# A decoder layer on one core: ScalarE copies the second turned head of each pair out of its bank

## The chip, the cores and the metric

One core of a Trainium2 chip runs the whole program. The metric is the device time in microseconds, the median of three runs of the same program. Beside it stands the profile of one execution, whose span (first to last instruction) is a little shorter than that execution's time.

## What is computed

A pre-norm decoder layer on x of (8, 256, 128) with a context of (8, 512, 128): self-attention with 16 heads of 64, one cross-attention head of 128, and a feed-forward part with quantised weights and activations, all in float32 to the outside.

```python
x = x + attn(layernorm(x), norm_scale, wq, wk, wv, w_out, b_out)      # 16 heads, softmax over 256 keys
x = x + xattn(k=ctx, v=ctx, q=layernorm(x), Wk, Wv, bv, Wq, bq, Wo, bo)  # softmax over 512 keys
x = x + ffn(layernorm(x), w1, b1, w2, b2)                             # 512 hidden, uint8 activations, int8 weights

def attn(x, ...):
    h = rmsnorm(x) * norm_scale
    q, k, v = (einsum('bsd,dhe->bshe', h, w) for w in (wq, wk, wv))
    p = softmax(einsum('bqhd,bkhd->bhqk', q * 64 ** -0.5, k))
    return einsum('bqhe,hed->bqd', einsum('bhqk,bkhd->bqhd', p, v), w_out) + b_out
```

## The kernel before

The program is written engine by engine: each engine has its own list of instructions in a fixed order, and semaphores tie the lists together. Nothing is scheduled by a compiler.

**The loop.** The work goes over 8 batches of 8 pairs of heads. One call of `step` on each engine stands for one pair j of batch b, with g = 8b + j as the running number of the pair. Batch 0 is written out ("first"), batches 1 to 6 are a loop of three rounds over two batches ("mid"), batch 7 is written out ("last"). After it comes a tail with the last batch's cross attention and the feed-forward part.

**One pair on the engines.** The heads are handled at different distances, so that every engine has work from several pairs in hand. In step g, TensorE turns (transposes) the scaled probabilities of the pair's two heads through the bank `turned_bank`, each turn four 128x128 matmuls on line 494; makes queries and keys of pair g+4 (L453 to L455, bank `q_bank`); projects the output of pair g-2 (`project_out`, L510, bank `acc_bank`); multiplies values of pair g-1 (L503, `o_bank`); and makes the scores of pair g+3 (L484, `score`). ScalarE takes exponentials of pair g+2 (L768), rounds q (`q_hi`, `split_hi`), copies `o_bank` to `oT`. VectorE takes the negated maxima of pair g+2 (L951), copies the turned probabilities to `pT` (L958), splits off q's remainder (`q_lo`, L943) and inverts sums (L955). GpSimd multiplies the probabilities by the inverted sums (L1324). All copies by ScalarE have line 759.

**Between them, side tasks.** A table gives up to three places in a step (0, 1, 2) to side tasks that go through `side_bank`: TH turns the normalised rows of the next batch, V0 and W1 to W3 make its values (`v_sb`), TC turns the context, TX turns the rows for the cross attention (ScalarE copies `x2T_hi`, VectorE then `x2T_lo`), QX, SX0 and SX1 its queries and scores (VectorE `x_negmax`, ScalarE `x_prob`), PX0 and PX1 turn its probabilities (ScalarE `x_pT_hi`, VectorE `x_pT_lo`), UX and OX finish it. TX has place 1 of pair 2. It is in batches 1 to 7, not in batch 0.

**The turned heads.** `turned_bank` is one bank. Both heads of a pair pass through it in turn: the even head's turn, its copy to `pT`, the odd head's turn, its copy. Both copies are VectorE's, counted by one semaphore, `pT_done`, and each turn waits for the copy before. In the last three pairs of the last batch (`late`) the turns go through three banks, `turned_bank` and the two `q_bank`s, by `turned_in`, and `copied_before` gives the count of copies that a turn must wait for. A pair's `values` in the next step read both copies.

**The order in a step.** On ScalarE: exponentials of the first head, side task of place 0, exponentials of the second head, `q_hi`, `oT`, side tasks of places 1 and 2. On VectorE: maxima of the first head, copy of the even turned head, maxima of the second, side task of place 0, inverse of the first sums, copy of the odd turned head, `q_lo`, side task of place 1, inverse of the second sums, side task of place 2. On TensorE: turn of the even head, q and k, side task of place 0, `project_out`, turn of the odd head, `values`, side task of place 1, scores, side task of place 2. At the end of pair 1 ScalarE also rounds the context rows (`c_rows_hi`), and in the last batch it scales the feed-forward weights there.

**The tail.** VectorE rounds and sums the feed-forward weights after its last copy, then adds the residual (L1002) from `acc_bank`, on which the rest of the cross attention hangs.

Of the kernel before, what the change touches and what calls it, by code (L numbers as in the profile page):

```python
# [71 lines left out]
def decoder_layer(nc, x, ctx_in, norm_scale, wq, wk, wv, w_out, b_out, xWk, xWv, xbv, xWq, xbq,  # L72
                  xWo, xbo, w1, b1, w2, b2, out):
    B, S, D = x.shape
    H, E = wq.shape[1], wq.shape[2]
# [5 lines left out]
    PAIRS = H // 2  # L81
# [32 lines left out]
    def wait(eng, sem, value):  # L114

        if isinstance(value, int) and value <= 0:
            return
        eng.wait_ge(sem, value)

    with ExitStack() as ctx:  # L120
# [6 lines left out]
        def sem(name):  # L127
            return ctx.enter_context(nc.semaphore(name))
# [56 lines left out]
        pT = sb("pT", [P, 4, QT, S])  # L185
# [102 lines left out]
        rinv_done = sem("rinv_done")  # L288
        prob_done = sem("prob_done")
        pT_raw = sem("pT_raw")  # L290
        pT_done = sem("pT_done")
        o_raw = sem("o_raw")
        o_done = sem("o_done")
        acc_raw = sem("acc_raw")
# [87 lines left out]
        def late(kind, j):  # L382

            return kind == "last" and j >= PAIRS - 3

        def turned_in(kind, j, r):
            if late(kind, j):
                return (turned_bank, *q_banks)[(2 * (j - PAIRS + 3) + r) % 3]
            return turned_bank

        def copied_before(kind, g, j, r):

            return 2 * g + r - (2 if late(kind, j) and (j > PAIRS - 3 or r) else 0)

        block = ctx.enter_context(nc.Block())

# [53 lines left out]
        def _(pe):  # L450
# [122 lines left out]
            def step(kind, b, parity, i, j):  # L573
                g = b * PAIRS + j
                pe.wait_ge(prob_done, 2 * g + 1)
                wait(pe, pT_done, copied_before(kind, g, j, 0))
                turn_probs(2 * j % 8, turned_in(kind, j, 0))
                if ahead(kind, j, 4):
                    if kind == "first" and j == 0:
                        pe.wait_ge(wqk_lo_done, 4)  # L580
                    project_qk((j + 4) % PAIRS, parity if j < PAIRS - 4 else 1 - parity, q_banks[j % 2])
                if task := side_at(kind, j, 0):
                    side(kind, b, 1 - parity, i, task)

                if not (kind == "first" and j < 1):
                    wait(pe, o_done, g - 1)
                if not (kind == "first" and j < 2):
                    if j == 2:
                        wait(pe, x1_done, b)
                    if kind == "first" and j == 2:  # L590
                        pe.wait_ge(load_wo, 16)
                    project_out((j - 2) % PAIRS)
                pe.wait_ge(prob_done, 2 * g + 2)
                pe.wait_ge(pT_done, copied_before(kind, g, j, 1))
                turn_probs(2 * j % 8 + 1, turned_in(kind, j, 1))
                if not (kind == "first" and j < 1):
                    if j == 1:
                        pe.wait_ge(side_free, side_index(kind, b, "W2") + 1)
                    if j == 5:
                        pe.wait_ge(side_free, side_index(kind, b, "W3") + 1)  # L600
                    if late(kind, j):
                        pe.wait_ge(pT_done, 2 * g)
                    slot = 2 * (j - 1) % 4
                    values((j - 1) % PAIRS, (slot, slot + 1), 1 - parity if j == 0 else parity)
                if task := side_at(kind, j, 1):
                    side(kind, b, 1 - parity, i, task)
                if ahead(kind, j, 3):
                    pe.wait_ge(q_lo_done, g + 4)
                    pe.wait_ge(exp_done, 2 * g + 6)
                    scores((j + 1) % 2)  # L610
                if task := side_at(kind, j, 2):
                    side(kind, b, 1 - parity, i, task)
# [29 lines left out]

            pe.wait_ge(pT_done, B * H)
            values(PAIRS - 1, (2, 3), LAST % 2, score_bank[0])
            pe.wait_ge(o_done, B * PAIRS - 1)
            project_out(PAIRS - 2)
# [108 lines left out]
        def _(act):  # L757
# [3 lines left out]
            def split_hi(parity, bank):  # L761

                return copy(q_hi[:, parity].rearrange("p r q -> p (r q)"), bank[:]).then_inc(q_hi_done, 1)
# [41 lines left out]
            def step(kind, b, parity, i, j):  # L805
                g = b * PAIRS + j
# [9 lines left out]
                if ahead(kind, j, 4):  # L816
                    act.wait_ge(q_raw, g + 5)
                    split_hi(j % 2, q_banks[j % 2])
                if not (kind == "first" and j < 1):
                    act.wait_ge(o_raw, g)  # L820
                    copy(oT[:, (j - 1) % 2], o_bank[:, 0:S]).then_inc(o_done, 1)
# [118 lines left out]
        def _(dve):  # L940
# [13 lines left out]
            def invert_sums(slot):  # L954
                nc.vector.reciprocal(rinv[:, slot], rowsum[:, slot]).then_inc(rinv_done, 1)  # L955

            def keep_turned(slot, bank):
                nc.vector.tensor_copy(pT[:, slot].rearrange("p k q -> p (k q)"), bank[:]).then_inc(pT_done, 1)  # L958

            def statistics(k, src, n):  # L960

# [119 lines left out]
            def step(kind, b, parity, i, j):  # L1081
                g = b * PAIRS + j
# [8 lines left out]
                if kind == "mid" and j == PAIRS - 1:  # L1091
                    aggregate(2, b, *PLAIN_NORM)
                dve.wait_ge(pT_raw, 2 * g + 1)
                keep_turned(2 * j % 4, turned_in(kind, j, 0))
                if kind == "first" and j == 0:
                    dve.wait_ge(exp_done, 3)
                    invert_sums(2)
# [24 lines left out]
                    residual(b, 1 - parity)  # L1122
                if kind == "mid" and j == PAIRS - 2:
                    statistics(2, x2_of(b), b)
                dve.wait_ge(pT_raw, 2 * g + 2)
                keep_turned(2 * j % 4 + 1, turned_in(kind, j, 1))
                if prepare and j == 0:
                    if kind == "first":
                        dve.wait_ge(load_x[1], 16)
# [293 lines left out]
```

## Time and profile before

| | us |
|---|---|
| median of 3 runs | 385.61 (385.21 to 386.19) |
| the profiled execution, its time | 386.2 |
| its span | 384.4 |
| TensorE matmul busy | 370.2 (96%) |
| VectorE busy | 325.8 (85%) |
| ScalarE busy | 259.6 (68%) |
| GpSimd busy | 174.3 (45%) |

The three runs lie within 0.3% of each other. The profiled execution is near the highest of them. A busy share says how long an engine had an instruction in hand, not whether anybody waited for it. Matmuls overlap one another on TensorE, so their start times tell more than their durations: a 128x128 matmul's row shows about 0.28 us, and the next one starts about 0.11 us later. A line with "PEld" is the weight load ahead of a matmul. What stands in square brackets at a row's end is how long the engine stood idle before it and who ended that.

### The profile page before, as it was taken

What the parts mean: (1) busy time and instruction counts of PE and PEld (TensorE: products, weight loads), DVE (VectorE), ACT (ScalarE), POOL (GpSimd) and SP (SyncE); (2) the same over time, 40 slices, a digit from 0 to 9 for tenths busy, and PEclk for the clock granted to TensorE, in tenths of its full rate; (3) what the DMA queues carried; (4) which work ended last, traced back from release to release, by engine and by line L of the source; (5) the groups of instructions that cost most, each with busy time, mean ns of one, the idle gap of its engine ahead of it and who ended that gap; (6) DMA issues with size and microseconds to landing.
All of it is one profiled execution on the core that took longest, in us unless ns stands there. A gap on an engine that the chain in (4) does not pass through costs nothing.

```text
span 384.4 us, 9135 instructions
## 1 busy us (share of the span) xinstructions
PE 370.2 (96%) x3034; PEld 288.4 (75%) x3034; DVE 325.8 (85%) x790; ACT 259.6 (68%) x812; POOL 174.3 (45%) x188
## 2 busy tenths in 40 slices
PE   8889999999999999999999999999999998999975
PEld 7768778778878877788777888787778876676422
DVE  3888879988998899879998899879987997876995
ACT  3867676766777567766677667756876668725664
POOL 2574435553555445545555454634555543521000
PEclk9999999999999999999999999999999999999999
DMA  7500000001000100001000100000000100000003
GB/s 231 166 15 2 2 0 2 3 3 41 2 1 3 42 0 0 0 0 41 0 0 0 41 0 0 0 30 10 0 0 0 27 2 2 2 2 0 2 0 109
DMA packets 7190, 7.50 MB, mean 20 GB/s; under 512 B 1280, under 2 KB 5120, under 8 KB 7168
## 3 DMA queue, kind: packets, MB, share of 16 engines
q1 hardware_dynamic: 6736, 6.69, 5.6%
q10 hardware_dynamic: 432, 0.52, 0.5%
q8 instruction: 13, 0.21, 0.2%
q14 instruction: 9, 0.07, 0.1%
HBM read 6.16 MB, written 1.05 MB: 19 GB/s over the span
## 4 chain that ended last, share of the span: by engine, by line
PE 81%; DVE 8%; ACT 7%; issue 3%; POOL 1%; POOLq 0%; DVEq 0%; ACTq 0%
PE o_bank L503 15%; PE turned_bank L494 14%; PE score L484 14%; PE acc_bank L510 7%; PE side_bank L453 4%; ACT prob L768 4%; PE q_bank L453 3%; PE q_bank L455 3%; PE q_bank L454 3%; PE side_bank L454 3%; PE side_bank L455 3%; PE side_bank L564 3%; DVE h_max L1280 2%; PE score L618 2%; PE side_bank L557 2%
## 5 line engine op out<-in xcount | busy, mean ns | idle before, releaser
L1324 POOL TENSOR_TENSOR prob<-prob,rinv 128x512 f32<-128x512 f32 x128 | 133.4, 1044 | 156.7 <-DVE rinv L955 156.4
L768 ACT ACTIVATE prob<-score,negmax 128x256 f32<-128x256 f32 x252 | 116.9, 473 | 36.2 <-DVE negmax L951 34.4
L958 DVE COPY pT<-turned_bank 128x512 f32<-128x512 f32 x124 | 84.1, 679 | 12.5 <-PE turned_bank L494 10.9
L951 DVE TENSOR_REDUCE negmax<-score 128x2 f32<-128x512 f32 x126 | 85.8, 682 | 3.4 <-PE score L484 1.1
L494 PE MATMUL turned_bank<-ident,prob 128*128 128x128 f32 x496 | 76.8, 277 | 0.3 <-DVE pT L958 0.2
L503 PE MATMUL o_bank<-pT,v_sb 128*64 128x256 f32 x504 | 68.3, 392 | 0.0
L494 PEld LDWEIGHTS turned_bank<-ident,prob 128*128 128x128 f32 x496 | 56.3, 141 | 9.1 <-issue 0.6
L768 ACT ACTIVATION_READ_ACCUMULATOR prob<-score,negmax 128x1 f32 x252 | 51.4, 204 | 0.0
L943 DVE TENSOR_TENSOR q_lo<-q_bank,q_hi 128x512 fp32r<-128x512 f32 x63 | 43.3, 689 | 6.8 <-ACT q_hi L759 4.9
L484 PE MATMUL score<-q_hi 64*128 64x256 f32 x252 | 42.3, 330 | 3.8 <-ACT prob L768 3.2
L503 PEld LDWEIGHTS o_bank<-pT,v_sb 128*64 128x64 f32 x504 | 30.5, 136 | 19.6 <-issue 9.2
L484 PEld LDWEIGHTS score<-q_hi 64*128 64x128 f32 x252 | 23.9, 184 | 25.8 <-issue 14.5
L453 PE MATMUL q_bank<-ht_hi,wqk_hi 128*128 128x256 f32 x124 | 40.2, 324 | 0.0
L510 PE MATMUL acc_bank<-wo_sb,oT 128*128 128x128 f32 x256 | 39.1, 276 | 0.0
L759 ACT ACTIVATE q_hi<-q_bank 128x512 fp32r<-128x512 f32 x63 | 38.1, 605 | 0.2
L759 ACT ACTIVATE v_sb<-side_bank 128x512 f32<-128x512 f32 x32 | 19.1, 598 | 26.6 <-PE side_bank L455 26.6
L510 PEld LDWEIGHTS acc_bank<-wo_sb,oT 128*128 128x128 f32 x256 | 34.7, 191 | 1.8 <-ACT oT L759 0.4
L484 PE MATMUL score<-q_lo,q_hi 64*128 64x256 f32 x252 | 35.9, 278 | 0.0
L484 PE MATMUL score<-q_hi,q_lo 64*128 64x256 f32 x252 | 35.8, 277 | 0.0
L455 PE MATMUL q_bank<-ht_hi,wqk_lo 128*128 128x256 f32 x124 | 34.9, 281 | 0.0
L454 PE MATMUL q_bank<-ht_lo,wqk_hi 128*128 128x256 f32 x124 | 34.8, 280 | 0.0
L759 ACT ACTIVATE oT<-o_bank 128x256 f32<-128x256 f32 x63 | 24.5, 388 | 6.2 <-PE o_bank L503 5.9
(249 smaller groups left out, 652.9 us busy)
## 6 DMA issues: line engine op xcount, KB each, us to landing
c_sb<-in_ctx_dram SPq DMA_DIRECT2D x8, 256.0 KB, 2.7
x_sb<-in_x_dram SPq DMA_DIRECT2D x8, 128.0 KB, 2.5
out_dram<-xn_all SPq DMA_DIRECT2D x4, 256.0 KB, 2.4
big<-in_L_attn_wk_dram ACTq DMA_DIRECT2D x2, 256.0 KB, 5.1
big<-in_L_attn_wq_dram SPq DMA_DIRECT2D x2, 256.0 KB, 5.6
big<-in_L_attn_wv_dram SPq DMA_DIRECT2D x2, 256.0 KB, 6.2
wo_sb<-in_L_attn_w_out_dram SPq DMA_DIRECT2D x1, 512.0 KB, 7.5
w_sb<-in_L_ffn_w_dram SPq DMA_DIRECT2D x2, 256.0 KB, 4.5
```

Source lines behind the costliest of these rows:

```text
L453: nc.tensor.matmul(dst, lhs_hi, rhs_hi, start=True, stop=False)
L454: nc.tensor.matmul(dst, lhs_hi, rhs_lo, start=False, stop=False)
L455: return nc.tensor.matmul(dst, lhs_lo, rhs_hi, start=False, stop=True)
L484: last = nc.tensor.matmul(banks[r][:, t * S:(t + 1) * S], query[rows, parity, 0, t * P:(t + 1) * P], key[rows, parity, 1, :], start=(n == ...
L494: last = nc.tensor.transpose(bank[:, kt * S + t * P:kt * S + (t + 1) * P], prob[:, slot, t, kt * P:(kt + 1) * P], ident[:])
L503: last = nc.tensor.matmul(bank[r * E:(r + 1) * E, 0:S], v_sb[:, vp, kt, h * E:(h + 1) * E], pT[:, slots[r], kt, :], start=(kt == 0), stop= ...
L510: last = nc.tensor.matmul(acc_bank[:, t * D:(t + 1) * D], oT[:, pair % 2, t * P:(t + 1) * P], wo_sb[:, pair, :], start=(pair == 0 and t == 0),
L759: return nc.scalar.activation(dst, src, ACT.Copy, **kw)
L768: last = nc.scalar.activation(prob[:, slot, t, :], banks[r][:, t * S:(t + 1) * S], ACT.Exp, bias=negmax[:, slot, t:t + 1], scale=1.0, accu ...
L951: nc.vector.tensor_reduce(negmax[:, slot], banks[r][:].rearrange("p (t k) -> p t k", k=S), X_AXIS, ALU.max, negate=True).then_inc(max_done, 1)
L958: nc.vector.tensor_copy(pT[:, slot].rearrange("p k q -> p (k q)"), bank[:]).then_inc(pT_done, 1)
L1324: nc.gpsimd.tensor_tensor(prob[:, slot], prob[:, slot], rinv[:, slot].unsqueeze(2).to_broadcast([P, QT, S]), ALU.mult).then_inc(prob_done, 1)
```

## The change

The copy of each pair's odd turned head moves from VectorE's list to ScalarE's. There it stands behind `q_hi` and ahead of `oT`. The even head's copy stays with VectorE. The one semaphore `pT_done` becomes two, `pT_even` (VectorE's copies) and `pT_odd` (ScalarE's), each of which rises by one per pair. `copied_before` returns two counts, and each turn, each late `values` and the last one wait for both. The operations and what they write are otherwise the same.

```diff
         def copied_before(kind, g, j, r):
 
-            return 2 * g + r - (2 if late(kind, j) and (j > PAIRS - 3 or r) else 0)
+
+            heads = r - (2 if late(kind, j) and (j > PAIRS - 3 or r) else 0)
+            return g + (heads + 1) // 2, g + heads // 2
...
                 pe.wait_ge(prob_done, 2 * g + 1)
-                wait(pe, pT_done, copied_before(kind, g, j, 0))
+                first, second = copied_before(kind, g, j, 0)
+                wait(pe, pT_even, first)
+                wait(pe, pT_odd, second)
                 turn_probs(2 * j % 8, turned_in(kind, j, 0))
...
                 if ahead(kind, j, 4):
                     act.wait_ge(q_raw, g + 5)
                     split_hi(j % 2, q_banks[j % 2])
+                act.wait_ge(pT_raw, 2 * g + 2)
+                copy(pT[:, 2 * j % 4 + 1].rearrange("p k q -> p (k q)"), turned_in(kind, j, 1)[:]).then_inc(pT_odd, 1)
                 if not (kind == "first" and j < 1):
                     act.wait_ge(o_raw, g)
                     copy(oT[:, (j - 1) % 2], o_bank[:, 0:S]).then_inc(o_done, 1)
...
                 if kind == "mid" and j == PAIRS - 2:
                     statistics(2, x2_of(b), b)
-                dve.wait_ge(pT_raw, 2 * g + 2)
-                keep_turned(2 * j % 4 + 1, turned_in(kind, j, 1))
```

ScalarE's list in the first batch of the loop, from the rounding of the context rows at the end of pair 1 to the end of pair 2, before:

```order
L759 ACTIVATE c_rows_hi<-c_sb 128x512
L809 ISA
L768 ACTIVATE prob,rowsum<-score,negmax 128x256 x2
L759 ACTIVATE ht_hi<-side_bank,scale_d 128x256
L814 REGISTER_ALU
L768 ACTIVATE prob,rowsum<-score,negmax 128x256 x2
L817 REGISTER_ALU
L759 ACTIVATE q_hi<-q_bank 128x512
L759 ACTIVATE oT<-o_bank 128x256
L782 REGISTER_ALU
L759 ACTIVATE x2T_hi<-side_bank 128x256
```

and the same stretch of the changed kernel, where the line numbers of later code are higher by 9:

```order
L768 ACTIVATE c_rows_hi<-c_sb 128x512
L818 ISA
L777 ACTIVATE prob,rowsum<-score,negmax 128x256 x2
L768 ACTIVATE ht_hi<-side_bank,scale_d 128x256
L823 REGISTER_ALU
L777 ACTIVATE prob,rowsum<-score,negmax 128x256 x2
L826 REGISTER_ALU
L768 ACTIVATE q_hi<-q_bank 128x512
L828 REGISTER_ALU
L768 ACTIVATE pT<-turned_bank 128x512
L768 ACTIVATE oT<-o_bank 128x256
L791 REGISTER_ALU
```

The copy to `pT`, with a register operation for its wait, has come in between `q_hi` and `oT`; `x2T_hi` follows `oT` as before.

VectorE's list from pair 2's `ht_lo` to pair 3's copy of the even turned head, before:

```order
L1012 SCALAR_TENSOR_TENSOR ht_lo<-side_bank,scale_d,ht_hi 128x256
L955 RECIPROCAL rinv<-rowsum 128x2
L1125 REGISTER_ALU
L958 COPY pT<-turned_bank 128x512
L1134 REGISTER_ALU
L943 TENSOR_TENSOR q_lo<-q_bank,q_hi 128x512
L943 TENSOR_TENSOR x2T_lo<-side_bank,x2T_hi 128x256
L955 RECIPROCAL rinv<-rowsum 128x2
L1087 ISA
L951 TENSOR_REDUCE negmax<-score 128x2
L1093 REGISTER_ALU
L958 COPY pT<-turned_bank 128x512
```

and in the changed kernel:

```order
L1023 SCALAR_TENSOR_TENSOR ht_lo<-side_bank,scale_d,ht_hi 128x256
L966 RECIPROCAL rinv<-rowsum 128x2
L1143 REGISTER_ALU
L954 TENSOR_TENSOR q_lo<-q_bank,q_hi 128x512
L954 TENSOR_TENSOR x2T_lo<-side_bank,x2T_hi 128x256
L966 RECIPROCAL rinv<-rowsum 128x2
L1098 ISA
L962 TENSOR_REDUCE negmax<-score 128x2
L1104 REGISTER_ALU
L969 COPY pT<-turned_bank 128x512
```

The first of the two `pT` copies has gone from the piece; `x2T_lo`, the maxima and the copy of pair 3's even head keep their order.

## Rows read from the trace of the kernel before

**Rows 1.** The page, busy time, share of the span and instructions of each engine
```profile
PE 370.2 (96%) x3034; PEld 288.4 (75%) x3034; DVE 325.8 (85%) x790; ACT 259.6 (68%) x812; POOL 174.3 (45%) x188
```

**Rows 2.** The page, the chain that ended last, shares by engine
```profile
PE 81%; DVE 8%; ACT 7%; issue 3%; POOL 1%; POOLq 0%; DVEq 0%; ACTq 0%
```

**Rows 3.** Groups of instructions: shapes, count, busy us, mean ns, idle before, releaser
```profile
L958 DVE COPY pT<-turned_bank 128x512 f32<-128x512 f32 x124 | 84.1, 679 | 12.5 <-PE turned_bank L494 10.9
...
L759 ACT ACTIVATE v_sb<-side_bank 128x512 f32<-128x512 f32 x32 | 19.1, 598 | 26.6 <-PE side_bank L455 26.6
```

**Rows 4.** Timeline, middle batch, pairs 1 to 3: start, duration, ScalarE then VectorE
```profile
149.00 0.60 ACT L759 ACTIVATE v_sb<-side_bank 128x512 f32<-128x512 f32 x1 [1.40 <-PE side_bank L455]
149.50 0.62 ACT L759 ACTIVATE c_rows_hi<-c_sb 128x512 fp32r<-128x512 f32 x1
...
152.71 0.41 ACT L759 ACTIVATE oT<-o_bank 128x256 f32<-128x256 f32 x1
152.97 0.43 ACT L759 ACTIVATE x2T_hi<-side_bank 128x256 fp32r<-128x256 f32 x1
154.59 0.48 ACT L768 ACTIVATE prob<-score,negmax 128x256 f32<-128x256 f32 x1 [1.20 <-DVE negmax L951]
...
149.95 0.67 DVE L958 COPY pT<-turned_bank 128x512 f32<-128x512 f32 x1
...
152.88 0.69 DVE L943 TENSOR_TENSOR q_lo<-q_bank,q_hi 128x512 fp32r<-128x512 f32 x1
153.49 0.41 DVE L943 TENSOR_TENSOR x2T_lo<-side_bank,x2T_hi 128x256 fp32r<-128x256 f32 x1
...
154.48 0.68 DVE L958 COPY pT<-turned_bank 128x512 f32<-128x512 f32 x1
```

**Rows 5.** Timeline, TensorE, second turns of pairs 2 and 3
```profile
150.18 0.61 PE L510 MATMUL acc_bank<-wo_sb,oT 128*128 128x128 f32 x4
...
150.74 0.14 PEld L494 LDWEIGHTS turned_bank<-ident,prob 128*128 128x128 f32 x1
150.78 0.30 PE L494 MATMUL turned_bank<-ident,prob 128*128 128x128 f32 x1
...
155.51 0.25 PEld L494 LDWEIGHTS turned_bank<-ident,prob 128*128 128x128 f32 x2
155.62 0.27 PE L494 MATMUL turned_bank<-ident,prob 128*128 128x128 f32 x1
```

**Rows 6.** Timeline, oT and the next first turn: a middle batch, the first batch
```profile
179.02 0.38 ACT L759 ACTIVATE oT<-o_bank 128x256 f32<-128x256 f32 x1
...
179.80 0.20 PEld L494 LDWEIGHTS turned_bank<-ident,prob 128*128 128x128 f32 x2
...
48.70 0.39 ACT L759 ACTIVATE oT<-o_bank 128x256 f32<-128x256 f32 x1
...
49.40 0.20 PEld L494 LDWEIGHTS turned_bank<-ident,prob 128*128 128x128 f32 x2
```

**Rows 7.** Timeline, last batch: pair 3's first copy and second turn, pair 4's PX0
```profile
323.55 0.68 DVE L958 COPY pT<-turned_bank 128x512 f32<-128x512 f32 x1
...
324.39 0.25 PEld L494 LDWEIGHTS turned_bank<-ident,prob 128*128 128x128 f32 x2
...
328.63 0.20 PEld L557 LDWEIGHTS side_bank<-ident,x_prob 128*128 128x128 f32 x2 [0.37 <-ACT x_prob L779]
```

**Rows 8.** Timeline, last batch, pair 5: last exponentials, oT, project_out's weights
```profile
335.59 0.49 ACT L768 ACTIVATE prob<-score,negmax 128x256 f32<-128x256 f32 x1
...
336.27 0.38 ACT L759 ACTIVATE oT<-o_bank 128x256 f32<-128x256 f32 x1
...
336.71 0.30 PEld L510 LDWEIGHTS acc_bank<-wo_sb,oT 128*128 128x128 f32 x2
```

**Rows 9.** Timeline, tail: the last projection and VectorE's residual
```profile
342.59 1.26 PE L510 MATMUL acc_bank<-wo_sb,oT 128*128 128x128 f32 x8
...
343.99 0.42 DVE L1002 TENSOR_TENSOR x_sb<-acc_bank,xb_sb 128x256 f32<-128x256 f32 x1
```

More of the change, by code:

```diff
@@ L290, in decoder_layer @@
         pT_raw = sem("pT_raw")
-        pT_done = sem("pT_done")
+        pT_even = sem("pT_even")
+        pT_odd = sem("pT_odd")
         o_raw = sem("o_raw")
@@ L593, in step @@
                 pe.wait_ge(prob_done, 2 * g + 2)
-                pe.wait_ge(pT_done, copied_before(kind, g, j, 1))
+                first, second = copied_before(kind, g, j, 1)
+                wait(pe, pT_even, first)
+                wait(pe, pT_odd, second)
                 turn_probs(2 * j % 8 + 1, turned_in(kind, j, 1))
@@ L601, in step @@
                     if late(kind, j):
-                        pe.wait_ge(pT_done, 2 * g)
+                        pe.wait_ge(pT_even, g)
+                        pe.wait_ge(pT_odd, g)
                     slot = 2 * (j - 1) % 4
@@ L641, in _ @@
             over_batches(pe, step)
-            pe.wait_ge(pT_done, B * H)
+            pe.wait_ge(pT_even, B * PAIRS)
+            pe.wait_ge(pT_odd, B * PAIRS)
             values(PAIRS - 1, (2, 3), LAST % 2, score_bank[0])
@@ L955, in invert_sums, with keep_first_turned @@
                 nc.vector.reciprocal(rinv[:, slot], rowsum[:, slot]).then_inc(rinv_done, 1)
-            def keep_turned(slot, bank):
-                nc.vector.tensor_copy(pT[:, slot].rearrange("p k q -> p (k q)"), bank[:]).then_inc(pT_done, 1)
+            def keep_first_turned(slot, bank):
+                nc.vector.tensor_copy(pT[:, slot].rearrange("p k q -> p (k q)"), bank[:]).then_inc(pT_even, 1)
             def statistics(k, src, n):
@@ L1093, in step @@
                 dve.wait_ge(pT_raw, 2 * g + 1)
-                keep_turned(2 * j % 4, turned_in(kind, j, 0))
+                keep_first_turned(2 * j % 4, turned_in(kind, j, 0))
                 if kind == "first" and j == 0:
```

## Prediction
> **What bounds the kernel now.** I read the page from the top: busy shares, then the chain that ended last, then the groups, and after that the timeline of one middle batch and of the last batch. TensorE is busy for 370.2 of 384.4 us, VectorE for 325.8 and ScalarE for 259.6 [rows 1]; the chain that ended last runs over PE for 81% and over VectorE and ScalarE for 15% [rows 2]. So VectorE's load is no price by itself: taking work from it gives time only where TensorE waits for VectorE, and giving work to ScalarE costs time only where TensorE ends up waiting for ScalarE. In the middle batches I looked for such places by the start times on PE. One is left: the second turn of pair 2. Four L510 matmuls begin at 150.18 and run 0.61 us in all, 0.28 each, so they start (0.61 - 0.28) / 3 = 0.11 apart and the turn could start at 150.62; it does at 150.78, its weights loaded at 150.74 [rows 5], **0.16 us** late. It waited for VectorE's copy of the first head, which ended at 149.95 + 0.67 = 150.62 [rows 4]; the release takes 0.12 us. At pair 3 the load (155.51) goes 0.11 ahead of its matmul (155.62), without a wait.
>
> **The moved copy.** 64 copies of 128x512 leave VectorE, 0.679 us each (43.5 us), and 64 come to ScalarE. The trace has no ScalarE copy of turned_bank; the nearest row is ScalarE's copy of another bank in the same shape, v_sb, 0.598 us [rows 3], and after it the next one starts 0.50 later (149.00, then the row after it at 149.50) [rows 4]. I take a slot of 0.49, with 0.48 and 0.52 as near bounds and VectorE's 0.68 as the far one. Most of the 64 have cover: ScalarE stands idle until VectorE has the next maxima, as for 1.20 us before 154.59, or until TensorE has a side task ready, as for 1.40 us before 149.00 [rows 4], and the copy goes into that hole. The Trainium skill ("ScalarE: Activation LUTs", Rules for kernel authors) tells one to use VectorE and not ScalarE for plain arithmetic, which speaks against this change. The rows here do not bear it out for a float32 bank: 0.598 us against 0.679. The same page (What ACT_TABLE_LOAD costs) has 186 ns + 0.833 ns per element, less 93 ns of overlap; an estimate from it is a slot of 0.52, and with it the sum below would be 0.2 us higher.
>
> **Who waits for the copy itself.** The next pair's first turn writes the same bank, so it now waits for ScalarE. The tightest places are where no side task stands between scores and turn. In pair 7 of a middle batch the new copy takes the place of oT, which starts at 179.02; it ends at 179.62, ScalarE's releases reach PE after 0.06 us (oT ends at 336.27 + 0.38 = 336.65, and the load that waits for it goes at 336.71 [rows 8]), so it is ready at 179.68 and the load goes at 179.80 [rows 6]. In pair 6 of the first batch it is ready at 48.70 + 0.60 + 0.06 = 49.36 and the load goes at 49.40 [rows 6]. Margins of 0.12 and 0.04: no cost, but thin. In the pairs with more side work between, the same subtraction leaves more. The extra wait instructions on PE (a second semaphore, six register operations in the loop body) stand in a queue that runs ahead of the array; I cost them at nothing, and if that cover were missing, rival 3 has the price.
>
> **What is queued behind the copy on ScalarE: pair 2.** Here the hole comes too late. From v_sb at 149.00 to x2T_hi at 152.97 ScalarE works back to back; the new copy goes in ahead of oT, so x2T_hi starts 0.49 later and ends at 152.97 + 0.43 + 0.49 = 153.89 [rows 4]. VectorE splits x2T (x2T_lo) before it takes the next scores' maxima and before it copies pair 3's first turned head. Before, x2T_lo started at 153.49, kept by q_lo (152.88 + 0.61); now it waits for x2T_hi, until about 153.93, a slip of 0.44 (I take 0.04 for the release to VectorE, a little under the 0.06 to PE above). Maxima and copy follow without a gap: the copy of pair 3's first head ends at 154.48 + 0.68 + 0.44 = 155.60, and its release reaches PE at 155.72. PE's load for the second turn went at 155.51 [rows 5]: now 155.72. A load that was waited for has its matmul 0.04 behind (150.74, 150.78), so the turn starts at 155.76 in place of 155.62: **0.14 us later**. The 0.16 that pair 2's second turn can gain, because VectorE's queue ahead of it holds one copy less, is inside this figure and is no gain: the chain from v_sb on ScalarE to the second turn of pair 3 is fixed by ScalarE, whatever PE does in between. Behind it PE is the bound again: pair 3's copy ahead of oT finds ScalarE's hole before x_prob. Six middle batches: 6 x 0.14 = **0.84 us**. Bounds: with slots of 0.48 and 0.52, 0.8 and 1.0; with a slip wholly hidden, -6 x 0.16 = -1.0; with VectorE's 0.68 as the slot, 6 x 0.33 = 2.0.
>
> **The last batch.** Pair 2 repeats this, with PE a little earlier against VectorE. The copy of pair 3's first head ends at 323.55 + 0.68 = 324.23, with a slip of 0.43 at 324.66, load at 324.78 in place of 324.39 [rows 7]. That is 0.39 for the load and 0.32 for the matmul, and further on it grows: in pair 4 PE waited 0.37 us for x_prob (load at 328.63 [rows 7]), and x_prob hangs on VectorE's maxima, which stand behind q_lo and so behind the whole slipped ScalarE row: **0.43 us**. In pair 5 PE loads project_out's weights at 336.71, 0.06 after oT's end at 336.27 + 0.38. oT started when its matmuls were done; ScalarE is free from about 336.04, shortly before the last exponential's end at 335.59 + 0.49. Now the odd copy starts there and oT 0.49 behind it, at 336.53: **0.26 us** more [rows 8]. Against that VectorE gets its copies off its queue before the weight sums: the first residual operation of the tail started at 343.99 right behind them, though acc_bank's last matmul ended at 343.85 [rows 9]; it can start at 343.91: **-0.08 us**. In the first batch I cost the move at nothing: there is no x2T in it, and its tightest turn has the margin of 0.04 above.
>
> **Sum.** 0.84 + 0.43 + 0.26 - 0.08 = 1.45 us. The profiled execution took 386.2 us (span 384.4 and 1.8 around it), so 387.65 for a like one; it is the highest of the three runs shown, and on their median of 385.61 I forecast **387.1 us**. That is 0.38% slower; a difference of about 0.3%, 1.16 us, is what a measurement of this kernel can tell from no change.
>
> **Rivals.** (1) *The slip is hidden and the stall comes back.* If x2T_hi doesn't hold VectorE up, because the copy's slot on ScalarE is short, PE keeps what it gains at pair 2's second turn. Pair 3's second turn was ready for its load at 155.16 + 0.12 = 155.28, 0.23 ahead; with PE 0.16 earlier 0.07 of that is left. With a slip under 0.07 the time would be 385.61 - 6 x 0.16 - 0.08 = 384.6, faster than before. For it: ScalarE's work on a bank is shorter than VectorE's. Against: the slip is a whole slot, and v_sb shows 0.50. (2) *It cancels.* The matmul would then be at 155.32 plus the slip, against 155.62: a slip of 0.30 costs a middle batch nothing, one of 0.2 gives it 0.1, and the last batch keeps some 0.5 us: 385.5 to 386.1, the middle 385.8. For it: my slip of 0.44 comes from rows with two decimals, and a middle batch costs only 0.14; 0.14 less of slip is enough. (3) *The first turns wait too.* If the copy takes longer than v_sb's, or the added waits and register operations on ScalarE and PE take room, the margins of 0.12 and 0.04 go. It decides at those margins. With 0.2 us more per copy, pair 7 loses 0.08 in each of 7 batches, three bare pairs of the first batch 0.16 each, and pair 2 loses 0.2 in each of 7: 0.56 + 0.48 + 1.4 = 2.4 us more than forecast, 389.5; with half of that 388.3, which I take as this case's time. Against: ScalarE's rows at this shape are 0.60 and 0.62 [rows 4]. (4) *The change doesn't do what it says*: the order shows all 64 copies on ScalarE and the rest unmoved, so this has no share.
>
> **How the numbers follow.** Forecast 0.55, no change (2) 0.27, stall gained (1) 0.07, first turns wait (3) 0.11. The forecast's own spread is that of a slot between 0.40 and 0.60: 0.09 less or 0.11 more in each middle batch and about 0.2 either way in the last, 386.4 to 388.0. The range takes that in, the case of no change, and the near half of (3) with most of the way to the far bound of the slot: 385.3 to 388.5. Slower by over 0.3% is above 386.77: most of the forecast's case (0.45 of its 0.55) and (3), 0.56. Faster by over 0.3% is below 384.45: only a lucky part of (1), 0.03. Within it 0.41.
>
> **What would show it.** In the profile after: the ScalarE group of pT copies, x64 or 62, near 0.6 us; in each middle batch x2T_lo starting 0.04 behind x2T_hi's end and waiting for it, not for q_lo; a wait of about 0.2 to 0.3 us on PE for VectorE's pT copy at the second turn of pair 3, and none at pair 2's; in the last batch a longer wait of PE for x_prob's successors and about 0.3 us before project_out in pair 5. VectorE near 282 us busy and ScalarE near 298. The forecast is wrong if oT and x2T_hi don't start later, if the wait at pair 3 is missing, or if the first turns wait for ScalarE.

## The result, and the profile after

The changed kernel takes **386.67 us** (median of 9 executions, 386.18 to 387.07) against 385.39 us for the kernel before beside it (9 executions, 385.10 to 386.19). The ratio is 1.0032, 95% interval 1.0021 to 1.0042: 0.3% slower, 1.3 us. A second comparison gave 386.45 against 385.73, ratio 1.0023 (1.0013 to 1.0033). The forecast was 387.1 us, slower, with a range from 385.3 to 388.5. Its sign and its main places were right; one size, that of the middle batches, was twice too large, and three small waits at first turns were not in it. The experiments end at a kernel that is 2 us faster than before.

Busy time and the chain that ended last, of the kernel after (compare [rows 1, 2]):

```profile
PE 370.4 (96%) x3034; PEld 287.6 (75%) x3034; DVE 288.5 (75%) x726; ACT 289.2 (75%) x876; POOL 174.6 (45%) x188
...
PE 81%; ACT 7%; DVE 6%; issue 3%; POOL 1%; POOLq 0%; DVEq 0%; ACTq 0%
```

VectorE's busy time fell by 37.3 us and ScalarE's rose by 29.6, and the time went up. TensorE's line is the same as before to 0.2 us. A balance of 288 to 289 us each looks better than 326 to 260, and says nothing about the end.

The groups of the two copies after (compare [rows 3]; columns: shapes and count | busy, mean ns | idle before, releaser), and VectorE's split of q:

```profile
L954 DVE TENSOR_TENSOR q_lo<-q_bank,q_hi 128x512 fp32r<-128x512 f32 x63 | 43.4, 691 | 41.4 <-ACT q_hi L768 41.4
...
L969 DVE COPY pT<-turned_bank 128x512 f32<-128x512 f32 x62 | 42.4, 684 | 10.1 <-PE turned_bank L497 10.0
...
L768 ACT ACTIVATE pT<-turned_bank 128x512 f32<-128x512 f32 x62 | 38.3, 618 | 1.2 <-PE turned_bank L497 1.2
```

62 copies of turned_bank are on each engine (and two of q_bank). ScalarE's take 618 ns against VectorE's 684. What VectorE was given back it spends waiting: 41.4 us ahead of q_lo, for ScalarE's q_hi, where it was 6.8 us before.

Next, ScalarE, VectorE and TensorE in pairs 2 and 3 of the middle batch that [rows 4, 5] show, after the change (timeline: start, duration, engine, operation, [idle before, releaser]):

```profile
148.04 0.60 ACT L768 ACTIVATE v_sb<-side_bank 128x512 f32<-128x512 f32 x1 [0.93 <-PE side_bank L458]
148.53 0.62 ACT L768 ACTIVATE c_rows_hi<-c_sb 128x512 fp32r<-128x512 f32 x1
149.05 0.47 ACT L777 ACTIVATE prob<-score,negmax 128x256 f32<-128x256 f32 x1
149.21 0.61 PE L513 MATMUL acc_bank<-wo_sb,oT 128*128 128x128 f32 x4
149.66 0.60 PE L497 MATMUL turned_bank<-ident,prob 128*128 128x128 f32 x4
...
151.69 0.64 ACT L768 ACTIVATE pT<-turned_bank 128x512 f32<-128x512 f32 x1
152.17 0.43 ACT L768 ACTIVATE oT<-o_bank 128x256 f32<-128x256 f32 x1
152.43 0.44 ACT L768 ACTIVATE x2T_hi<-side_bank 128x256 fp32r<-128x256 f32 x1
152.90 0.42 DVE L954 TENSOR_TENSOR x2T_lo<-side_bank,x2T_hi 128x256 fp32r<-128x256 f32 x1 [0.34 <-ACT x2T_hi L768]
153.31 0.67 DVE L962 TENSOR_REDUCE negmax<-score 128x2 f32<-128x512 f32 x1
153.90 0.68 DVE L969 COPY pT<-turned_bank 128x512 f32<-128x512 f32 x1
154.04 0.61 PE L513 MATMUL acc_bank<-wo_sb,oT 128*128 128x128 f32 x4
154.66 0.42 PEld L497 LDWEIGHTS turned_bank<-ident,prob 128*128 128x128 f32 x4 [0.20 <-POOL prob L1333]
154.69 0.63 PE L497 MATMUL turned_bank<-ident,prob 128*128 128x128 f32 x4
```

The stall at pair 2's second turn is gone: the turn starts at 149.66, as soon as the projection's four matmuls, 0.11 apart from 149.21 on, let it (149.21 + 0.44 = 149.65). At pair 3 there is a new one: projection at 154.04, the turn at 154.69 where 154.48 was possible. On the way stands what the prediction named: the copy's slot ahead of oT (151.69 to 152.17, 0.48 us), a late x2T_hi, x2T_lo waiting for it, maxima, copy, load. The releaser printed at 154.66, GpSimd's prob, had ended at 154.52; VectorE's copy ended at 153.90 + 0.68 = 154.58 and is the last. The two ends lie close together, and both hang on x2T_lo, so this was worth a second look: TensorE's sequencer had a semaphore instruction open there, for the two counts of copies and not for prob. It ran from 153.494 to 154.630, 0.05 us behind the copy's end, and the load went 0.025 us after it. So the name beside a wait for several semaphores must be read against the rows.

**Where the time went**, in nanoseconds. I paired the matmuls of the two traces one by one and took the difference of their start times at the borders of the stages; each column is what a stage adds to or takes from the kernel before. (The middle column is the mean of six periods of the loop; the border ahead of it lies before the first batch's last pair. The first and the last column are not the change: up to 12 us each trace has its own start-up, and the feed-forward part its own clock. That the start-up is not the change's can be seen from the column itself: the kernels "behind x2T" and "oT first" have all odd copies on ScalarE too, and differ from the kernel before by 31 and 177 ns there, not by 1.1 us.)

```
kernel             to 12 us   first   one middle   last    tail    feed-
                   (not the   batch   batch, x6    batch   norm    forward
                   change)
after              -1165      +40     +70          +728    -37     +547
after, again       -1142      +20     +49          +702    -47      -11
both on VectorE     -449      -13     -56           +21    +37       +4
pair 1 alone       -1102        0     -173          +20    +30       -7
pair 2 alone       -1435       +7     +110         +461    +37     +460
all but pair 2     -1033      +42     -172         +293    -36       +4
behind x2T           -31     +234     +344         +837    -46      -10
oT first (last)     -177      +14     +52          +440    -47       -3
pair 1, scalings 6   +24      -20     -173        -1214   +422       -5
pair 1, scalings 5  -300       -6     -173        -1213    +26       -3
```

The change itself is 0.04 + 6 x 0.07 + 0.73 - 0.04 = 1.15 us in the first trace and 0.97 us in the second, against 1.28 and 0.72 us between the medians. For all ten rows the sum without the two outer columns lies within 0.5 us of the difference of the medians. The 0.55 us in the feed-forward part is variation: the second trace of the same kernel doesn't have it. The granted clock tells them apart (stretch and its length, busy us of PE, PEld, DVE, ACT and POOL with counts, PEclk, DMA share, GB/s). After:

```profile
370.00:384.00 14.00, 8.64 (x39) 4.04 (x38) 9.01 (x26) 6.68 (x10) 0.00 (x0) 0.87 0.21 73
```

After, again:

```profile
370.00:384.00 14.00, 7.68 (x38) 3.63 (x38) 8.84 (x26) 6.45 (x10) 0.00 (x0) 1.00 0.22 75
```

The same number of matmuls is busy for 8.64 us at a mean granted clock of 0.87 and 7.68 at 1.00, that is, at the higher of TensorE's two levels (2.4 GHz) for all of the stretch.

### The profile page after: what moved, and what is told of

It reads as the page before. It is cut to its first block, busy times and chain, and to the rows that moved or that the text cites. A ratio compares the mean times of both kernels' runs of the same rounds, so it can differ in the third digit from the quotient of the medians.

```text
span 384.9 us, 9156 instructions
## 1 busy us (share of the span) xinstructions
PE 370.4 (96%) x3034; PEld 287.6 (75%) x3034; DVE 288.5 (75%) x726; ACT 289.2 (75%) x876; POOL 174.6 (45%) x188
## 4 chain that ended last, share of the span: by engine, by line
PE 81%; ACT 7%; DVE 6%; issue 3%; POOL 1%; POOLq 0%; DVEq 0%; ACTq 0%
PE o_bank L506 15%; PE turned_bank L497 14%; PE score L487 14%; PE acc_bank L513 7%; ACT prob L777 4%; PE side_bank L456 4%; PE q_bank L456 3%; PE q_bank L458 3%; PE q_bank L457 3%; PE side_bank L457 3%; PE side_bank L458 3%; PE side_bank L567 3%; DVE h_max L1289 2%; PE side_bank L560 2%; PE score L626 1%
## 5 line engine op out<-in xcount | busy, mean ns | idle before, releaser
L954 DVE TENSOR_TENSOR q_lo<-q_bank,q_hi 128x512 fp32r<-128x512 f32 x63 | 43.4, 691 | 41.4 <-ACT q_hi L768 41.4
L969 DVE COPY pT<-turned_bank 128x512 f32<-128x512 f32 x62 | 42.4, 684 | 10.1 <-PE turned_bank L497 10.0
L768 ACT ACTIVATE pT<-turned_bank 128x512 f32<-128x512 f32 x62 | 38.3, 618 | 1.2 <-PE turned_bank L497 1.2
```

What stands on the lines that cost most here:

```text
L768: return nc.scalar.activation(dst, src, ACT.Copy, **kw)
L954: return nc.vector.tensor_tensor(dst, whole, hi.bitcast(F32), ALU.subtract)
```

## The experiments

My theory, A, was: the copies don't cost by their sum; pair 1's gives time back, pair 2's takes it away through x2T_hi, and pair 5's in the last batch through oT. The rival, B: the extra semaphore, or the copies' mass on ScalarE, slows every pair a little. (Where a later kernel has another alternative, its expectation says so.) Each kernel is a variant of the changed one in which a predicate says whose second copy is ScalarE's; VectorE makes the others where it did before, and releases the second semaphore. Each is compared with executions of the kernel before that were made beside it, in three sets, whose medians are 385.76, 385.73 and 385.42 us.

**Both copies on VectorE, two semaphores.** This leaves only the change's bookkeeping.

```diff
+        def odd_by_act(kind, j):
+            return False
...
+                if odd_by_act(kind, j):
                     act.wait_ge(pT_raw, 2 * g + 2)
                     copy(...).then_inc(pT_odd, 1)
...
+                if not odd_by_act(kind, j):
+                    dve.wait_ge(pT_raw, 2 * g + 2)
+                    keep_second_turned(2 * j % 4 + 1, turned_in(kind, j, 1))
```

> Both copies stay with VectorE, and only the semaphore is split in two, so that TensorE has the changed kernel's waits and register operations. Theory A (the time comes from the place of the copy in ScalarE's and VectorE's queues): no change from the kernel before, 385.4 us within 0.3. Theory B (the added waits on TensorE cost): up to the whole 1.3 us of the change, 386.7.

Measured: 385.53 us against 385.76, ratio 0.9996 (0.9987 to 1.0005). The extra waits cost nothing that the comparison can tell. The trace even shows a gain, 0.056 us in every middle batch, at one place, pair 2's second turn:

```profile
149.37 0.68 DVE L974 COPY pT<-turned_bank 128x512 f32<-128x512 f32 x1
149.59 0.61 PE L517 MATMUL acc_bank<-wo_sb,oT 128*128 128x128 f32 x4
150.10 0.42 PEld L501 LDWEIGHTS turned_bank<-ident,prob 128*128 128x128 f32 x4
150.10 0.55 PE L501 MATMUL turned_bank<-ident,prob 128*128 128x128 f32 x3
```

The copy ends at 150.05 and the turn's load goes 0.05 later; before, it ended at 150.62 and the load went at 150.74 [rows 4, 5], 0.12 later. What differs is a wait instruction of its own on TensorE's sequencer, a kind of record that the timeline leaves out. From the trace, in ns (start, duration):

```
before:            150667   51  EVENT_SEMAPHORE
                   150744  138  LDWEIGHTS turned_bank<-ident,prob
two semaphores:    149490   51  EVENT_SEMAPHORE
                   150100  138  LDWEIGHTS turned_bank<-ident,prob
after, pair 5 of    39518   51  EVENT_SEMAPHORE
the first batch:    39593  142  LDWEIGHTS turned_bank<-ident,prob
after, pair 3 of   153494 1136  EVENT_SEMAPHORE
a middle batch:    154655  138  LDWEIGHTS turned_bank<-ident,prob
```

Where the semaphore instruction has not begun when the copy ends, it starts 0.04 us after that end and the load 0.076 us behind it, 0.11 to 0.12 in all. Where it went long before, the load itself waited and goes 0.05 after the end. The last pair of records is a third case: the instruction carries two semaphores, began 1.1 us before the copy's end (154.584) and lasted until 0.05 us after it; from that end to the load it is 0.07. So 0.065 of the 0.16 us stall of before was the way of waiting and not the copy: the load goes 0.052 after the copy's end in place of 0.117. The turn's first matmul starts 0.09 earlier and the later ones 0.06, of which 0.056 us a batch are left. That the compiled order of the waits decides this is my reading of the records; no run changed the order of the waits alone.

**Pair 1 alone on ScalarE** (8 of 64 copies). The edit is `return j == 1` in the predicate.

> Only the odd copy of pair 1 of every batch goes to ScalarE. Theory A: VectorE reaches pair 2's maxima and first copy earlier, the stall at pair 2's second turn goes, in each of six middle batches 0.18 us (0.153 + 0.026, read from the start times of the changed kernel against those of the kernel before), and x2T_hi isn't behind the copy, so nothing is given back: 385.4 - 1.07 = 384.3 us. Theory B (each copy on ScalarE costs, by contention or by its waits): 8 of 64 copies, 385.4 + 0.2 = 385.6.

Measured: 385.23 against 385.76, ratio 0.9982 (0.9972 to 0.9992). It is faster, against theory B, but the medians show 0.5 us where theory A had 1.07: the interval is 0.3 to 1.1 us, and the eleven executions fall into two groups, 384.0 to 384.4 and 385.2 to 385.4. The trace has 0.99: every middle batch is 0.173 us shorter and nothing is given back there. ScalarE and VectorE in pair 1, then pair 2's second turn:

```profile
145.76 0.61 ACT L772 ACTIVATE pT<-turned_bank 128x512 f32<-128x512 f32 x1
145.92 0.69 DVE L959 TENSOR_TENSOR q_lo<-q_bank,q_hi 128x512 fp32r<-128x512 f32 x1 [0.53 <-ACT q_hi L772]
148.34 0.67 DVE L974 COPY pT<-turned_bank 128x512 f32<-128x512 f32 x1
148.75 0.61 PE L517 MATMUL acc_bank<-wo_sb,oT 128*128 128x128 f32 x4
149.20 0.49 PE L501 MATMUL turned_bank<-ident,prob 128*128 128x128 f32 x3
```

The copy of pair 2's first head ends at 149.01, and the load (at 149.09) is 0.11 ahead of its matmul, without a wait: 148.75 + 0.44 = 149.19, the matmul at 149.20. All of what the change can win in the middle batches is in this one copy of eight.

**Pair 2 alone** (`return j == 2`).

> Only the odd copy of pair 2 of every batch goes to ScalarE. Theory A: x2T_hi, x2T_lo, the maxima and pair 3's first copy slip by 0.38 to 0.44, pair 3's second turn waits, 0.10 to 0.14 us in each of six middle batches, with pair 2's stall of before still there; in the last batch 0.43 us more: 385.4 + 1.1 to 1.3 = 386.6 us. That is nearly the whole loss of the change by one eighth of its copies. Theory B: 8 of 64 copies, 385.6.

Measured: 386.68 against 385.76, ratio 1.0030 (1.0019 to 1.0041), with 8 of 64 copies 0.92 us, the whole of the change's loss within the intervals. A middle batch is 0.110 us longer than before and 0.166 longer than with both copies on VectorE. The wait is there, in 7 batches (total us, times, longest):

```profile
DVE x2T_lo L959 <- ACT x2T_hi L772: 2.4, 7, 0.3
```

**All but pair 2** (`return j != 2`, 56 of 64 copies on ScalarE).

> The changed kernel with pair 2's odd copy given back to VectorE, 56 of 64 copies on ScalarE. Theory A: the stall at pair 2's second turn is gone (-1.07), nothing slips at pair 3, the first batch's thin turns keep +0.06, the last batch keeps the later projection of pair 5 (+0.27) and the tail's -0.05: 385.4 - 0.8 = 384.6 us. Theory B: seven eighths of the loss, 386.5.

Measured: 384.99 against 385.76, ratio 0.9985 (0.9975 to 0.9995). By the trace, a middle batch is 0.172 us shorter, as with pair 1 alone: six more copies per batch on ScalarE cost it nothing. This speaks against the rival of the mass and for the one row of ScalarE. The last batch keeps 0.293, at project_out of pair 5.

**Pair 2's copy behind oT and x2T_hi**: if x2T_hi is what costs, one can let it go first (all other pairs as changed).

```diff
+                if odd_by_act(kind, j) and j != 2:
                     act.wait_ge(pT_raw, 2 * g + 2)
                     copy(...).then_inc(pT_odd, 1)
                 if not (kind == "first" and j < 1):
                     act.wait_ge(o_raw, g)
                     copy(oT[:, (j - 1) % 2], o_bank[:, 0:S]).then_inc(o_done, 1)
...
+                if j == 2:
+                    act.wait_ge(pT_raw, 2 * g + 2)
+                    copy(...).then_inc(pT_odd, 1)
```

> The changed kernel, but in pair 2 of every batch ScalarE copies the odd turned head behind oT and x2T_hi and not ahead of them. Theory A (what stands behind the copy in ScalarE's queue and who waits for the copy both count): x2T_hi slips no more, so pair 3's second turn waits for nothing, but the copy starts two slots of 0.26 us later, is ready about 0.45 us after pair 3's first turn wants the bank, and TensorE waits there: per middle batch -0.18 + 0.45 = +0.27 us in place of +0.07, 385.6 + 1.6 + 0.7 for the first and last batch = 387.9 us, slower than the changed kernel by about 1.1. Theory B (x2T_hi's slip is all that the copy costs in pair 2): the middle batches keep -0.18 us each, 385.6 - 1.07 + 0.3 = 384.8.

Measured: 388.52 against 385.73, ratio 1.0077 (1.0060 to 1.0094): 2.8 us, the dearest place of all. It is more than theory A's 2.3 or so: 0.344 us in each middle batch, where 0.27 was expected, and 0.23 in the first batch, whose pair 3 waits for the copy behind oT as well. ScalarE and TensorE at pair 3's first turn:

```profile
153.56 0.43 ACT L772 ACTIVATE oT<-o_bank 128x256 f32<-128x256 f32 x1
153.82 0.44 ACT L772 ACTIVATE x2T_hi<-side_bank 128x256 fp32r<-128x256 f32 x1
154.09 0.66 ACT L772 ACTIVATE pT<-turned_bank 128x512 f32<-128x512 f32 x1
154.86 0.42 PEld L501 LDWEIGHTS turned_bank<-ident,prob 128*128 128x128 f32 x4 [0.65 <-issue]
154.89 0.63 PE L501 MATMUL turned_bank<-ident,prob 128*128 128x128 f32 x4 [0.48 <-ACT pT L772]
```

Now the first turn, which writes the same bank, waits for the copy: the copy ends at 154.75, the load goes at 154.86. ScalarE's row in pair 2 is full for both: whichever of the two goes second is waited for. This is the mechanism of rival 3, made on purpose.

**oT of pair 5 ahead of the copy, in the last batch only**, the rest as changed.

```diff
+                behind = kind == "last" and j == 5
+                for part in (("oT", "odd") if behind else ("odd", "oT")):
```

> The changed kernel, but in pair 5 of the last batch ScalarE copies oT ahead of the odd turned head. Theory A: the 0.27 us that the trace of the changed kernel shows at the projection behind oT of that pair is gone, and nothing else moves: the changed kernel's time less 0.27, 386.6 us; the start times on TensorE must show it where the median can't. Theory B (the projection is late there because the whole last batch is late): no change at that place.

Measured: 386.59 against 385.73, ratio 1.0020 (1.0009 to 1.0031). The changed kernel beside it has 386.45, so the medians do not show the gain (0.14 us more and not 0.27 less, with executions that spread over 1.1 us each). The traces do: the last batch adds 0.440 in place of 0.728 and 0.702, which is the term alone. The rows of pair 5, first after the change, then with oT first:

```profile
335.34 0.49 ACT L777 ACTIVATE prob<-score,negmax 128x256 f32<-128x256 f32 x1
335.79 0.62 ACT L768 ACTIVATE pT<-q_bank 128x512 f32<-128x512 f32 x1
336.27 0.41 ACT L768 ACTIVATE oT<-o_bank 128x256 f32<-128x256 f32 x1
336.73 0.52 PEld L513 LDWEIGHTS acc_bank<-wo_sb,oT 128*128 128x128 f32 x4 [0.39 <-ACT oT L768]
```

```profile
336.17 0.49 ACT L781 ACTIVATE prob<-score,negmax 128x256 f32<-128x256 f32 x1
336.86 0.38 ACT L772 ACTIVATE oT<-o_bank 128x256 f32<-128x256 f32 x1
337.14 0.59 ACT L772 ACTIVATE pT<-q_bank 128x512 f32<-128x512 f32 x1
337.30 0.52 PEld L517 LDWEIGHTS acc_bank<-wo_sb,oT 128*128 128x128 f32 x4
```

From the last exponential to project_out's load it is 1.39 us after the change and 1.13 with oT first; before it was 1.12 [rows 8].

**The changed kernel once more**, beside these.

> The changed kernel once more, on the same chip as the three others. Theory A: 1.003 of the kernel before, 386.9 us; in the trace the same shifts per batch (+0.07 us), and other times only in the first 12 us and the feed-forward part, where the two traces at hand differ by up to 1.4 and 0.5 us. Theory B (the 0.5 us more in the feed-forward part belongs to the change): it is there again, with the granted clock under the kernel before's there.

Measured: 386.45 against 385.73, ratio 1.0023 (1.0013 to 1.0033), 0.4 us under the 386.9 expected. In its trace a middle batch is 0.049 us longer, the last 0.702, and the extra time in the feed-forward part is gone, which decides for theory A.

**Pair 1 alone, and the last batch's weight scalings later.** The traces showed a larger hole that has nothing to do with the copies. In the last batch ScalarE scales five weight blocks for the feed-forward part, ahead of pair 2's exponentials. Of the kernel before:

```profile
317.74 1.88 ACT L759 ACTIVATE w_t<-w_sb,w_inv 128x128 f32<-128x128 f32 x5
...
321.57 0.39 PE L484 MATMUL score<-q_hi 64*128 64x256 f32 x2 [1.13 <-ACT prob L768]
```

TensorE waits 1.13 us for ScalarE behind them. I moved them, first to the end of pair 6.

```diff
-                if kind == "last" and j == 1:
+                if kind == "last" and j == 6:
```

> Only pair 1's odd copies on ScalarE, and in the last batch the five scalings of feed-forward weights go from the end of pair 1 to the end of pair 6. In the kernel before they take 1.88 us of ScalarE ahead of pair 2's exponentials, and TensorE waits 1.13 us for these; in pair 6 ScalarE stands idle for 2.2 us. Theory A: 384.7 (pair 1 alone) less 1.1 = 383.6 us, faster than both kernels. Theory B (the wait moves to VectorE's rounding of the weights or to pair 3 of that batch): 384.7.

Measured: 383.75 against 385.73, ratio 0.9944 (0.9928 to 0.9960). The last batch is 1.214 us shorter, but 0.39 us come back in the tail: the scalings now end just ahead of VectorE's rounding of them, which stands ahead of the norm that TensorE waits for.

```profile
337.74 1.88 ACT L772 ACTIVATE w_t<-w_sb,w_inv 128x128 f32<-128x128 f32 x5
339.65 0.43 DVE L1095 TENSOR_SCALAR w_q<-w_t 128x512 f16<-128x512 f32 x1 [0.39 <-ACT w_t L772]
345.08 0.44 PE L679 MATMUL acc_bank<-ident,xn 128*128 128x128 f32 x2 [0.66 <-DVE xn L1002]
```

So, one pair earlier (`j == 5`):

> As the kernel with pair 1's copies alone on ScalarE and the weights scaled at the end of pair 6, but with the weights at the end of pair 5 of the last batch. In that kernel's trace VectorE's rounding waited 0.39 us for the weights and TensorE's xn turn of the tail came 0.38 us later; ScalarE stands idle for 2.26 us behind pair 5's oT (334.40 to 336.67), and the five scalings take 1.88. Theory A: the 0.38 is won back and nothing else moves, 383.75 - 0.38 = 383.4 us, 0.9935 of the kernel before. Theory B (the room behind oT is too short, oT of pair 6 slips): the projection behind it comes later by up to 0.3, 383.7.

Measured: **383.37 us** (5 executions, 383.00 to 383.76) against 385.42, ratio 0.9943 (0.9930 to 0.9957). It is faster than both kernels, by 2.05 us than the one before. The gain of the last batch stays, and the tail adds 0.026 us in place of 0.422. (Its advantage over the version with pair 6, 0.40 us in the traces' tails, is not told apart by the ratios, whose intervals overlap.) The rows:

```profile
333.71 0.38 ACT L772 ACTIVATE oT<-o_bank 128x256 f32<-128x256 f32 x1
333.99 1.88 ACT L772 ACTIVATE w_t<-w_sb,w_inv 128x128 f32<-128x128 f32 x5
336.36 0.38 ACT L772 ACTIVATE oT<-o_bank 128x256 f32<-128x256 f32 x1 [0.49 <-PE o_bank L510]
338.87 0.42 DVE L1095 TENSOR_SCALAR w_q<-w_t 128x512 f16<-128x512 f32 x1
```

The scalings stand behind oT and end at 335.87, 0.49 us before ScalarE has anything else to do, and VectorE's rounding at 338.87 waits for nothing. That is a test both of the place they go to and of the one they leave.

## Why the prediction was right, and where it was not

**What bounds the kernel**: right. TensorE's stalls are the whole account. Without pair 2, 56 copies on ScalarE made no middle batch longer than 8 copies did.

**The copy's size**: right. The slot was taken at 0.49 us and is 0.48 (151.69 to 152.17). The far bound, 0.68, was never near. On the Trainium skill ("ScalarE: Activation LUTs", What ACT_TABLE_LOAD costs) the prediction had an estimate of 0.52 for the slot; the trace has 0.04 less. The same page (Rules for kernel authors) sends `add` and `mul` to VectorE, and gives VectorE's speed in bf16 as the reason. It does not name copies, and these are float32: 618 ns on ScalarE against 684 on VectorE.

**Busy times**: off. ScalarE was to be near 298 us and is 289.2, VectorE near 282 and is 288.5. I had added and taken away durations. Operations that follow one another overlap at their ends, and the busy line counts an overlap once: (325.8 - 288.5) / 64 = 0.58 us per copy for VectorE and (289.2 - 259.6) / 64 = 0.46 for ScalarE, close to the distances between starts (153.90 to VectorE's next operation at 154.50, 0.60, and 0.48) and not to the durations. No term of the sum used these.

**First turns that wait for ScalarE's copy**: no cost forecast, 0.02 to 0.04 us measured at each of three. The margin of 0.12 in pair 7 of the middle batches held. In the first batch the turns behind the copies of pairs 4 and 6 start 0.06 and 0.05 later, of which 0.035 and 0.023 stay: the copy of pair 4 ended at 39.48 and the load went at 39.59, 0.11 later, where I had taken 0.06 for ScalarE's release. The load was behind a semaphore instruction of its own (39.518 in the listing above). For pair 6 my margin of 0.04 was counted with the same 0.06. The step that failed is the one price for all releases. The third place I did not look at: in the last batch pair 3's first turn waits for the copy of pair 2, which stands behind the exponentials that the weight scalings hold up, and 0.04 stays. Of the kernel after:

```profile
321.10 0.62 ACT L768 ACTIVATE pT<-turned_bank 128x512 f32<-128x512 f32 x1
...
321.83 0.42 PEld L497 LDWEIGHTS turned_bank<-ident,prob 128*128 128x128 f32 x4 [0.18 <-issue]
```

With pair 2's copy back on VectorE this last wait is gone, and with pair 2's alone on ScalarE it is there.

**Pair 2, the middle batches**: the right chain, **the mis-sized term**. Forecast +0.14 us a batch, 0.84 in all; measured +0.07 and +0.05, 0.42 and 0.29. Counted from v_sb's start, on which the chain hangs: x2T_lo started 153.49 - 149.00 = 4.49 behind it before [rows 4] and 152.90 - 148.04 = 4.86 after, a slip of 0.37, not 0.44; the turn 155.62 - 149.00 = 6.62 [rows 4, 5] and 154.69 - 148.04 = 6.65, 0.03 later, not 0.14. From the turn's second matmul on it is 0.05, and in the first of the two traces a further 0.01 comes at the next side task, which waits for VectorE's qx_lo. Two things are missing from my sum. ScalarE's row was not back to back by itself: before, pair 2's first exponentials at 150.06 had waited for VectorE's maxima (149.35 + 0.68 = 150.03), behind the copy that the change took away; after, they start at 149.05, 0.52 behind c_rows_hi in place of 0.56. And the release from VectorE's copy to the load is 0.07 (154.584 to 154.655), not 0.12, which I had measured at a place where the semaphore instruction began only behind the copy. The claim that pair 2's own gain is inside the figure holds for the most part: against the run with two semaphores, pair 1's copy gives 0.117 us a batch; with pair 2's copy on ScalarE too, of that only 0.04 to 0.06 is left (+0.110 with pair 2 alone, +0.070 and +0.049 with all).

The two rows of the kernel before that this rests on:

```profile
149.35 0.68 DVE L951 TENSOR_REDUCE negmax<-score 128x2 f32<-128x512 f32 x1
...
150.06 0.47 ACT L768 ACTIVATE prob<-score,negmax 128x256 f32<-128x256 f32 x1
```

The exponentials can't start before the maxima's end, and did right behind it.

**The last batch**: right. Forecast 0.43 + 0.26 = 0.69. Measured, by the first matmul of each stage: 0.08 at pair 3's first turn (the wait above, which the forecast didn't have), 0.20 more at its second turn, 0.17 ahead of x_prob's turn, that is 0.45; and 0.27 at project_out of pair 5; 0.73 with what is small. So over half of the change's cost lies in one batch of eight, and the run with oT first showed the second part alone.

**The tail**: forecast -0.08, measured -0.04. The residual started at 343.99, 1.40 behind the last projection's start [rows 9]; now it is 1.36, since it follows the last matmul's end (343.88) by 0.09 and not by the 0.06 that I had taken:

```profile
342.61 1.27 PE L513 MATMUL acc_bank<-wo_sb,oT 128*128 128x128 f32 x8
...
343.97 0.42 DVE L1013 TENSOR_TENSOR x_sb<-acc_bank,xb_sb 128x256 f32<-128x256 f32 x1 [0.75 <-issue]
```

**The rivals.** Rival 2, that it cancels, was the near miss: a middle batch lost half of what I forecast, for a reason of the kind I had named (0.14 less slip would do), and the last batch kept the result above the bound. Rival 1 wanted a hidden slip and did not occur; all but pair 2 is what it would look like (384.99). Rival 3 occurred in a small form: the waits at three first turns above cost 0.10 us together, and came from the price of a release and not from a longer copy; the run with the copy behind x2T_hi shows what it costs where there is no margin.

**How much of the fit is luck.** The forecast's sum was 1.45 us, the traces have 1.15 and 0.97. The middle batches fell 0.42 to 0.55 short of it. The waits at first turns, which I had at nothing, and the smaller gain in the tail made up some 0.14 of that.

## What to carry to other kernels

When one engine bounds, moving work off a busy engine pays only where the bound engine waits for it: look up which single instruction that is, and move that one. Here 1 of 8 copies held all the gain of the middle batches, another one of the 8 nearly all of the loss, and the other six nothing. Before a step goes onto another engine's queue, list what stands behind it there until the next idle time, and who waits for each of those; a step with no idle time behind it delays all of them by its slot. And when looking for a hole for one change, read the longest waits of the bound engine as well: the 1.13 us one in the last batch was worth more than the change in question.

## What the runs showed of the hardware

A release to TensorE had three prices in these traces, from a copy's end to the waiting load: 0.052 us where the load carried the wait (both copies on VectorE), 0.071 where a semaphore instruction with two semaphores had already begun and was still open (after, pair 3's second turn), and 0.113 to 0.117 where the semaphore instruction began only after the copy's end (from VectorE before, from ScalarE after). More waits are not dearer by themselves: splitting one semaphore in two let the load at this place go 0.065 us sooner.

A ScalarE copy of a 128x512 float32 bank takes a slot of 0.48 us and a VectorE copy of the same 0.60 (the kernel after).

The two traces of the changed kernel differ by 0.56 us in the feed-forward part, at mean granted clocks of 0.87 and 1.00. Up to 12 us the eleven traces lie up to 1.5 us apart, these two 0.02; what sets that was not looked into. Spans should not be subtracted to judge a change of 1 us; start times paired at stage borders can be.
